# Narrow causal attention: undivided probabilities are transposed, and the value product is multiplied by inverted sums that TensorE spreads over a bank

## The reference, cut to what matters

```
q = (h @ wq); k = (h @ wk); v = (h @ wv)      # q and k rotated
scores = q . k / 8;  scores = where(causal, scores, -1e30)
attn = softmax(scores)
o = attn @ v
x = x + o @ wo ...
```

## Time and profile before

| | us |
|---|---|
| median of three timed runs | 3975.33 (3968.56 to 3976.48) |
| the profiled execution | 3977.27 |
| its span, first to last instruction | 3975.5 |
| TensorE busy | 3386.8 (85%) |
| VectorE busy | 2620.2 (66%) |
| ScalarE busy | 1915.0 (48%) |
| GpSimd busy | 993.6 (25%) |

### The profile page before, as it was taken

One profiled execution on the slowest core, in us unless ns is written; L12 is line 12 of the kernel. 1 busy time (PEld: TensorE's weight loads), 2 busy tenths in 40 slices (PEclk: granted clock), 3 DMA queues, 4 the chain that ended last, 5 costly groups with the idle time before them and its releaser, 6 DMA issues. The chain is left out here.

```text
span 3975.5 us, 62571 instructions
## 1 busy us (share of the span) xinstructions
PE 3386.8 (85%) x21000; PEld 2236.6 (56%) x21002; DVE 2620.2 (66%) x8701; ACT 1915.0 (48%) x5261; POOL 993.6 (25%) x960
## 2 busy tenths in 40 slices
PE   6899999887798698997889999988599567999976
PEld 4566666655454333343666666655355346788864
DVE  6777878665343677774777777766444367777765
ACT  4566666554222166665466666655322113555541
POOL 3212112232344100111221212123244342222213
PEclk9899999888899589998889999988799768999986
DMA  3320400011754422111150310001275600000010
GB/s 120 107 99 22 139 1 1 18 45 42 200 89 81 101 54 54 45 24 40 47 198 7 115 46 1 1 33 42 97 161 91 140 14 1 14 14 4 1 32 22
DMA packets 203909, 234.62 MB, mean 59 GB/s; under 512 B 20358, under 2 KB 190280, under 8 KB 202824
## 3 DMA queue, kind: packets, MB, share of 16 engines
q1 hardware_dynamic: 172648, 190.48, 15.8%
q0 software_dynamic: 30944, 40.14, 6.0%
HBM read 96.03 MB, written 133.73 MB: 58 GB/s over the span
## 5 line engine op out<-in xcount | busy, mean ns | idle before, releaser
L1896 DVE CUSTOM_DVE_ANT_0 bank<-bank,p_mask 128x256 f32<-128x256 f32 (+3 forms) x1280 | 583.4, 489 | 248.1 <-PE bank L1469 221.1
L1726 ACT ACTIVATE p_prob<-bank,p_small 128x256 f32<-128x256 f32 (+3 forms) x1280 | 649.4, 520 | 174.3 <-DVE p_small L1896 167.4
L1731 ACT ACTIVATE p_prT<-bank 128x512 f32<-128x512 f32 x752 | 429.1, 605 | 460.1 <-PE bank L1478 442.1
L2241 POOL TENSOR_TENSOR p_tm<-p_rope_a,p_rope_b 128x512 f32<-128x512 f32 x192 | 246.2, 1282 | 1407.6 <-DVE p_rope_b L1875 1360.4
L1469 PE MATMUL bank<-p_k,p_q 64*128 64x256 f32 (+3 forms) x3840 | 534.4, 353 | 17.9 <-ACT p_prob L1726 16.7
L1478 PE MATMUL bank<-g_ident,p_prob 128*128 128x128 f32 x3008 | 454.7, 292 | 78.5 <-ACT p_v L1712 36.7
L1478 PEld LDWEIGHTS bank<-g_ident,p_prob 128*128 128x128 f32 x3008 | 344.6, 146 | 173.9 <-issue 46.8
L1487 PE MATMUL bank<-p_prT,p_v 128*64 128x512 f32 (+1 forms) x1504 | 425.9, 609 | 0.3 <-ACT p_prT L1731 0.3
L1905 DVE TENSOR_SCALAR p_prob<-p_prob,p_small 128x256 f32<-128x256 f32 (+3 forms) x1280 | 416.5, 389 | 11.3
L1469 PEld LDWEIGHTS bank<-p_k,p_q 64*128 64x128 f32 (+1 forms) x3840 | 344.3, 192 | 117.1 <-issue 66.4
L1942 DVE TENSOR_REDUCE p_nmax<-bank 128x1 f32<-128x512 f32 x512 | 325.1, 685 | 95.2 <-PE bank L1528 89.5
(11 more groups left out here) (289 smaller groups left out, 6243.5 us busy)
## 6 DMA issues: line engine op xcount, KB each, us to landing
sorted<-p_blank SPq DMA_DIRECT2D x32, 2304.0 KB, 18.9
p_w<-in_L_ffn_w SPq DMA_DIRECT2D x96, 256.0 KB, 4.4
p_h_in<-sorted SPq DMA_DIRECT2D x158, 144.0 KB
p_k_st<-k_saved SPq DMA_DIRECT2D x16, 288.0 KB
p_q_st<-q_saved SPq DMA_DIRECT2D x16, 288.0 KB
g_stage<-in_L_ffn_wq SPq DMA_DIRECT2D x8, 512.0 KB, 4.4
g_stage<-in_L_ffn_wo SPq DMA_DIRECT2D x16, 256.0 KB, 5.2
second_sum<-g_res SPq DMA_DIRECT2D x8, 512.0 KB, 6.1
```

The source lines that it names most:

```text
L1726: act.activation(s.prob.ap[:, 0:s.o.w], s.use.ap[:, 0:s.o.w], ACT.Exp, bias=sm[:, 0, j:j + 1], scale=-1.0, accum_out=sm[:, 1, j:j + 1]).th ...
L1731: act.activation(s.prT.ap, s.use.ap, ACT.Copy).then_inc(s.use.free[0].sem)
L1896: dve.tensor_tensor_reduce(x, x, A.mask[:, A.mask.shape[1] - o.w:], -1.0, FAR, ALU.add, ALU.min, o.sm.ap[:, 0, h.j:h.j + 1]).then_inc(made)
```

## The change

In the narrow attention the multiplication of the probabilities is gone. "invert" writes the inverted sums of a group (4 for each query) to a buffer that both groups of a tile share, and the transposes wait for the exponentials alone. Ahead of the value product TensorE now takes one more bank of the ring and fills it with eight matmuls: the stationary operand is one column of inverted sums, repeated to 64 columns, the moving operand the identity, so that the bank holds each head's inverted sum of query n in column n, in all 64 rows of the head. ScalarE copies the value product to SBUF ("divide"), VectorE multiplies it by the new bank. In a new step "parts", later in the same step of the unit, ScalarE rounds that to the high part, from SBUF, and GpSimd subtracts for the low part. The rings of high and low parts have one buffer in place of two.

In both attentions the copy of the values is moved: it is issued one piece earlier, with the key and value product, and waits for that product alone; VectorE's rotation of the keys waits for the copy, and frees the bank.

```diff
@@ -350,3 +350,6 @@
         prT = Ring([sb(f"prT{i}", [P, KV * P])[:, :] for i in range(8)])
-        oT_hi, oT_lo = (Ring([sb(f"oT_{s}{i}", [P, KV * P], F32R)[:, :] for i in range(2)]) for s in ("hi", "lo"))
+        oT_hi, oT_lo = (Ring([sb(f"oT_{s}{i}", [P, KV * P], F32R)[:, :] for i in range(2 if wide else 1)]) for s in ("hi", "lo"))
+        if not wide:
+            oT = Ring([sb("oT", [P, KV * P])[:, :]])
+            inverse = Ring([sb(f"inverse{i}", [P, nk, KV])[:, :, :] for i in range(3)])
         small = Ring([sb(f"small{i}", [P, 3, KV])[:, :, :] for i in range(3)])
@@ -414,6 +417,8 @@
             w_used[c] = kb.full
+            v = self.step("v_copy", A)
+            v.t, v.kb, v.v, v.made = t, kb, unit.v, self.scalar_made.up()
+            unit.v_made.append(v.made)
             yield
             k = self.step("k_rotate", A)
-            k.t, k.kb, k.qb, k.ra, k.rb, k.tm = t, kb, qb, s.ra, s.rb, s.tm
-            k.rotated = self.vector_made.up()
+            k.t, k.kb, k.qb, k.ra, k.rb, k.tm, k.v_made = t, kb, qb, s.ra, s.rb, s.tm, v.made
             k.q_sum, k.k_sum = self.pool_made.up(), self.pool_made.up()
@@ -422,10 +427,4 @@
             rotated[t] = s.tm, k.k_sum
-            if wide:
-                yield
-            v = self.step("v_copy", A)
-            v.t, v.kb, v.v, v.rotated = t, kb, unit.v, k.rotated
-            unit.v_made.append(kb.free)
             yield
-            if not wide:
-                yield
+            yield
 
@@ -488,2 +487,14 @@
 
+        def invert(o):
+            s = self.step("invert", A)
+            if o.g == 0:
+                o.inverse = inverse.take()
+            else:
+                o.inverse = pend[-1].inverse
+            s.o, s.exps, s.inverse = o, o.exps, o.inverse
+            o.inverted = self.vector_made.up()
+            o.sm.users.append(o.inverted)
+            o.norms = o.exps
+            o.prT, o.prT_made = [], []
+
         def turn(o, kt):
@@ -499,4 +510,9 @@
             s = self.step("weigh", A)
-            s.os, s.use, s.hi, s.lo = os, wring.take(), oT_hi.take(), oT_lo.take()
-            s.hi_made = self.scalar_made.up()
+            s.os, s.spread = os, None
+            if not wide:
+                s.spread, s.inverse, s.inverted = wring.take(), os[0].inverse, [o.inverted for o in os]
+                s.inverse.users.append(s.spread.full)
+            s.use = wring.take()
+            if wide:
+                s.hi, s.lo, s.hi_made = oT_hi.take(), oT_lo.take(), self.scalar_made.up()
             for o in os:
@@ -508,5 +524,19 @@
 
+        def divide(wd):
+            s = self.step("divide", A)
+            s.use, s.spread = wd.use, wd.spread
+            s.x = wd.x = oT.take()
+
         def low_parts(wd):
-            s = self.step("low_parts", A)
-            s.use, s.hi, s.lo, s.hi_made = wd.use, wd.hi, wd.lo, wd.hi_made
+            if wide:
+                s = self.step("low_parts", A)
+                s.use, s.hi, s.lo, s.hi_made = wd.use, wd.hi, wd.lo, wd.hi_made
+                wd.made = wd.use.free
+            else:
+                s = self.step("parts", A)
+                s.x, s.divided = wd.x, wd.spread.free
+                s.hi, s.lo = wd.hi, wd.lo = oT_hi.take(), oT_lo.take()
+                s.hi_made, s.lo_made = self.scalar_made.up(), self.pool_made.up()
+                wd.x.users.append(s.lo_made)
+                wd.made = s.lo_made
             return wd
@@ -517,3 +547,3 @@
             s.o, s.hi, s.lo, s.use = o, wd.hi, wd.lo, wring.take()
-            s.ready = [wd.use.free, o_ready[o.c]]
+            s.ready = [wd.made, o_ready[o.c]]
             wd.hi.users.append(s.use.full)
@@ -579,3 +609,3 @@
                 if prev:
-                    normalise(prev)
+                    (normalise if wide else invert)(prev)
                 beside()
@@ -583,3 +613,3 @@
                 if weighed:
-                    weighed = low_parts(weighed)
+                    (low_parts if wide else divide)(weighed)
                 if wide:
@@ -597,2 +627,4 @@
                     scores(cur, 2)
+                elif weighed:
+                    low_parts(weighed)
                 beside()
...
@@ -1482,2 +1516,9 @@
             first = s.os[0]
+            if s.spread:
+                w.wait_ge(s.spread.before, *s.inverted)
+                for j in range(KV):
+                    for g in range(A.nk):
+                        ins = pe.matmul(s.spread.ap[cols(g * A.hd, A.hd), j * P:(j + 1) * P],
+                                        s.inverse.ap[:, g, j:j + 1].to_broadcast([P, A.hd]), ident[:, :], start=True, stop=True)
+                ins.then_inc(s.spread.full[0].sem)
             w.wait_ge(s.use.before)
@@ -1710,4 +1751,4 @@
         elif s.kind == "v_copy":
-            w.wait_ge(s.rotated, s.v.after)
-            act.activation(s.v.ap[:, s.t, :], s.kb.ap[:, KW:2 * KW], ACT.Copy).then_inc(s.kb.free[0].sem)
+            w.wait_ge(s.kb.full, s.v.after)
+            act.activation(s.v.ap[:, s.t, :], s.kb.ap[:, KW:2 * KW], ACT.Copy).then_inc(made)
 
@@ -1732,3 +1773,3 @@
 
-        elif s.kind == "weigh":
+        elif s.kind == "weigh" and A.wide:
             w.wait_ge(s.use.full, s.hi.after)
@@ -1736,2 +1777,10 @@
 
+        elif s.kind == "divide":
+            w.wait_ge(s.use.full, s.x.after)
+            act.activation(s.x.ap, s.use.ap, ACT.Copy).then_inc(s.use.free[0].sem)
+
+        elif s.kind == "parts":
+            w.wait_ge(s.divided, s.hi.after)
+            act.activation(s.hi.ap, s.x.ap, ACT.Copy).then_inc(made)
+
         elif s.kind == "small_bias":
@@ -1871,2 +1920,4 @@
             w.wait_ge(use.full, A.const, s.ra.after)
+            if s.kind == "k_rotate":
+                w.wait_ge(s.v_made)
             dve.tensor_tensor(a, x, c_all, ALU.mult)
@@ -1874,4 +1925,3 @@
             dve.tensor_tensor(b[:, :, 0:hf], x[:, :, hf:hd], s_left, ALU.mult)
-            ins = dve.tensor_tensor(b[:, :, hf:hd], x[:, :, 0:hf], s_right, ALU.mult)
-            ins.then_inc(s.qb.free[0].sem if s.kind == "q_rotate" else made)
+            dve.tensor_tensor(b[:, :, hf:hd], x[:, :, 0:hf], s_right, ALU.mult).then_inc(use.free[0].sem)
 
@@ -1907,2 +1957,11 @@
 
+        elif s.kind == "invert":
+            o = s.o
+            w.wait_ge(*s.exps, s.inverse.after)
+            dve.reciprocal(s.inverse.ap[:, o.g, :], o.sm.ap[:, 1, :]).then_inc(made)
+
+        elif s.kind == "divide":
+            w.wait_ge(s.spread.full, s.use.free)
+            dve.tensor_tensor(s.x.ap, s.x.ap, s.spread.ap, ALU.mult).then_inc(s.spread.free[0].sem)
+
         elif s.kind == "low_parts":
@@ -2244,3 +2303,3 @@
                     for x in (s.ra, s.rb))
-            w.wait_ge(s.rotated)
+            w.wait_ge(s.kb.free)
             w.wait_ge(own.turn())
@@ -2248,2 +2307,7 @@
 
+        elif s.kind == "parts":
+            w.wait_ge(s.hi_made, s.lo.after)
+            w.wait_ge(own.turn())
+            pool.tensor_tensor(s.lo.ap, s.x.ap, s.hi.ap.bitcast(F32), ALU.subtract).then_inc(made)
+
         elif s.kind == "small_bias":
```

More of the change, by code:

```diff
@@ L621, in attention @@
             project_out(settled)
-        if full:
-            project_out(low_parts(weigh(full)))
-        normalise(prev)
+        (normalise if wide else invert)(prev)
         for kt in range(prev.nkt):
             turn(prev, kt)
-        project_out(low_parts(weigh(pend + [prev])))
+        for os in ([full] if full else []) + [pend + [prev]]:
+            weighed = weigh(os)
+            if not wide:
+                divide(weighed)
+            project_out(low_parts(weighed))
         self.routing = itertools.chain(*routing)
```

## The result

The changed kernel takes 4370.4 us (4366.4 to 4373.5, four runs) where the kernel before took 3975.9 (3968.6 to 3989.7, four runs) on the same chip: 1.099 times as long (95% interval 1.0955 to 1.1019), 394 us slower. The forecast was 4306 in a range of 4110 to 4480.

A forecast was written before the change was run, and what follows sets the result against it. TensorE was taken to set the pace of steady units. From 3977: +234 for steady and normalising units, +34 router units, -15 VectorE's relief, +78 clock gave 4308, or 4306 for the timed median; range 4110 to 4480.

The forecast's parts named there:

- early copy of the values: Steady unit: step 0's 1.12 us wait goes; 0.51 and 0.80 go too, already inside the late projections' differences.
- The low part behind the exponentials: Projections early in even steps wait for rounding and GpSimd's subtraction behind late exponentials: 6.69 us a steady unit.
- The spread: Float32 matmuls ahead of each value product, column groups side by side: 0.86 us each, 3.44 a unit on TensorE.
- serial rival: The spread's two column groups follow each other on TensorE: 110 us more, 4416; chance 0.11.
- The spread's bank: Bank held until VectorE's multiplication, needed by the step's first turn: costed at nothing, upper end 0.5 us a unit.
- The clock: TensorE's granted clock in steady units falls from 1.00 to 0.92, costing 3 us a unit, 78 in all.
- VectorE's relief: Dropped multiplications free VectorE in router and normalising units: worth between 0 and 104 us, taken as 15.
- Router units: Six units with the router: half of 6.69 counted for late projections, +5.7 us each, +34 in all.
- Normalising units: Four units beside a later batch's normalisation, counted like steady ones: +9.0 us each, plus 3 for the clock.
- The wide attention: ScalarE stands at the copy of the values ahead of exponentials: taken as 0, with 15 us either way.
- in time: Rival: low part is ready while TensorE does the spread; about 3995 us with the clock full; chance 0.11.
- VectorE the pacemaker: Faster rival: VectorE paces the ten router and normalising units; 8 us a unit gives 3929; chance 0.09.

The follow-up runs named there:

- E1: Kernel before with only the copy of the values issued one piece earlier: 3912.9 us, ratio 0.985.
- E5: Changed kernel with copy at the value product, "parts" right behind the multiplication, and every spread done twice (16 matmuls for 8): 4066.0 us, ratio 1.026.
- E3: Changed kernel with ScalarE's copy of the value product put back where the product is issued, "parts" still late: 4313.8 us, ratio 1.0865.
- E8: Changed kernel with 14 needless matmuls filling TensorE's wait ahead of three of a unit's four projections: 4246.8 us, ratio 1.0715.
- E2: Changed kernel with "parts" (rounding and low part) put right behind the multiplication, ahead of the scores of heads 2 and 3: 4052.4 us, ratio 1.021.
- E7: Changed kernel with the low part subtracted on VectorE in place of GpSimd, at the same late place: 4416.4 us, ratio 1.115.
- E6: E1 with the probabilities' scaling left out in the narrow attentions, so the softmax is not divided there: 3854.4 us, ratio 0.9735.
- E4: Changed kernel with the edits of E2 and E3 together: 3978.1 us, ratio 1.002.

## Why the prediction was right, step by step

The direction, the place and the mechanism were right; the forecast was 65 us short. The steady unit was put at 61.2 us at full clock and 64.2 with the clock's loss; it is 66.3. The first and third rows are in waits proper: the forecast's 6.69 counted how much later projections start, and the old waits of 0.51 and 0.80 us lay inside it. By steps, in us a steady unit:

| step | predicted | measured | from |
|---|---|---|---|
| early copy of the values | -2.43 (alone) | -2.5 | E1 |
| spread, four times | +3.44 | +3.5 | E5 |
| low part late, at the projection | +8.0 (6.69 + 0.51 + 0.80) | +6.4 | waits after |
| spread's bank held | 0 (to 0.5) | +2.2 | waits after, E3 |
| clock | +3 | about +4 | E8 |
| sum | +12.0 | +13.6, of 14.1 in all | windows |

- *The low part behind the exponentials* held. The signs named for it are in the trace: waits of 1.86, 2.17 and 2.26 us with GpSimd's subtraction as releaser, though 13 and not 16 in four units. E2 shows that the place alone makes them, and E7 that the engine doesn't. Term by term the forecast's starts, with the old waits added, make waits of 2.50, 2.35, 2.17 and 0.98 us in steps 2, 4, 6 and 0; measured are 2.17, 2.26, 1.86 and 0.24, the last 0.71 where step 7 doesn't wait (E3).
- *The spread* held: 0.86 us was forecast, the trace shows 0.85 us of loads and E5 0.76 to 0.88. The serial rival falls: one behind the other, 16 passes of 0.108 us would be 1.7. The Trainium skill, in "TensorE: Matmul & The Clock Gate", Part 3 (Packing small matmuls), lets weight loads overlap matmuls in flight only where the row group differs. These tiles differ in columns alone, and 16 loads in 0.85 us speak against the rule here.
- *The spread's bank* is the step that failed. The prediction looked at what TensorE does between the multiplication and the bank's next use, and costed the hold at nothing. It didn't follow the copy ahead of the multiplication, which moved from "weigh" to "divide" and so behind "beside" and two exponentials on ScalarE. The prediction did follow the rounding past the exponentials of heads 2 and 3; it left out that the copy was moved past those of heads 0 and 1. E3 takes that wait away, and the kernel gains 49 us of the 65 that were missing.
- *The clock* was taken at 0.92, and 0.92 is what the window shows. It was the middle of two bounds, so that it was hit is in part luck. Its price was a microsecond too low: with E8's 4 us for 26 units it is 104 in place of 78. This and E3's 49 overlap, since the wait of step 7 is one of those that cost clock.
- *VectorE's relief* was put at 15 of 0 to 104 us. Without the other parts it is 45 (E6), some 36 of it in the ten router and normalising units. What of it is left in the changed kernel, where TensorE waits for other things, no run tells apart.
- *Router units* were put at +5.7 each and grew by 39 / 6 = 6.5. *Normalising units* were put at the steady unit's +12 and grew by 35 / 4 = 8.8. So the 65 us are a difference: steady units 46 over the forecast (310 for 264), normalising ones 13 under it, router ones with the relief 20 over it, and 12 outside these units, which no run explains. *The wide attention* was put at 0 and has the same units; the 3.10 us of the earlier trace rows were an idle ScalarE on no path.
- The rival *in time* is E4 in the flesh: forecast 3995, measured 3978, with 52.7 us a unit where the prediction named 53 as the sign of a misjudged chain. *VectorE the pacemaker* asked for 8 us in each of the ten router and normalising units, and its relief gives 3.6 (E6); the quickest form of the whole change (E4) isn't faster than the kernel before.

So the change loses 394 us like this, in points of ratio: early copy -1.5, spread and multiplication less the relief +1.7 (E4), and +9.7 for the two late places, of which about 2.7 are the clock's (E8).

## What to carry to other kernels

When a step is moved in a list that all engines walk, follow every instruction of it on its own engine's queue to what now stands ahead of it there, and from there to each buffer that it frees: here ScalarE, about half idle, was late all the same, because it takes its instructions in order. Try the members of such a chain (copy, multiply, round, subtract) directly behind the work that feeds them, and compare part by part: here one part of the change was worth 1.5% by itself, and the rest, even when well placed, gave it back. On TensorE a wait can cost more than its length. Four waits a unit, 8.5 us in all, cost about half as much again by the clock's fall behind them (4 us); where only one wait of 2.2 us a unit was left, the steady windows show 0.98 (E2) and 0.99 (E8).

## What the runs showed of the hardware

- Behind 13 of 17 waits of 1.8 to 2.3 us, each between stretches of dense work, TensorE's granted clock fell to half (0.51 in the windows at 587 and 611), and doing needless matmuls in three of four made the kernel 108 us faster (E8).
- Float32 matmuls of two column groups (128x64 stationary, 128 moving columns), with one column of 128 values repeated to 64 as the stationary operand, took 0.054 us a record, 16 in 0.85 us and 32 in 1.73. The value product, with dense operands, has a pair of records for 512 columns every 0.43 us, which is 0.054 for 128 columns as well.
- A 128x512 subtraction took 1.27 us on GpSimd; a multiplication of that size took 0.69 on VectorE with one operand in PSUM.
